# Windowed attention stack on one Trainium2 core: norms of q and k apart, softmax tail moved within VectorE's slot

## The reference

```python
def attn_layer(x, Wqkv, qs, ksc, Wo):              # x is shifted by one token in its upper half of channels
    q, k, v = heads(x @ Wqkv)                      # 16 heads of 64, INNER = 1024
    q = q / max(|q|, 1e-12) * qs                   # |.| over the 64 of a head
    k = k / max(|k|, 1e-12) * ksc
    q = q * cos * scale + rotate_half(q) * sin * scale
    k = k * cos / scale + rotate_half(k) * sin / scale
    out = local_attention(q, k, v)                 # windows of 32 tokens see themselves and the window before
    return out @ Wo
def ffn_layer(x, g, b, W1, b1, W2, b2):            # layer norm, then a gated GELU of 341
    a, gate = split(layernorm(x) * g + b @ W1 + b1)
    return (a * gelu(gate)) @ W2 + b2
for i in range(6):
    x = attn_layer(shift(x), ...) + x
    x = ffn_layer(shift(x), ...) + x
```

## Time and profile before

| | us |
|---|---|
| median of 3 runs | 4362.35 (4358.89 to 4362.66) |
| the profiled execution | 4365.13 |
| its span | 4363.3 |
| PE busy | 3866.2 (89%) |
| DVE busy | 3296.5 (76%) |
| ACT busy | 2534.1 (58%) |
| POOL busy | 2498.8 (57%) |

### The profile page before, as it was taken

The page is one execution under the profiler, slowest core; times in us unless marked ns, Lnnn a source line. Parts: engine busy times, 40 slices in busy tenths (PEclk is TensorE's granted clock), DMA queues, the critical chain, the costliest instruction groups (busy, mean ns, idle before and its releaser), DMA issues. The chain is left out here.

```text
span 4363.3 us, 151598 instructions
## 1 busy us (share of the span) xinstructions
PE 3866.2 (89%) x66488; PEld 2314.4 (53%) x66488; DVE 3296.5 (76%) x4385; ACT 2534.1 (58%) x3236; POOL 2498.8 (57%) x2036
## 2 busy tenths in 40 slices
PE   6887799999999999999778877899999999999997
PEld 3323456665665666665433334566666666666664
DVE  7997777888888787888454436788888878878884
ACT  6885456566665666666324444556566565666654
POOL 0001677777777777777100005786777777777773
PEclk8999999999999999999789998999999999999998
DMA  0001232332323233222000002323323223232221
GB/s 19 1 1 42 72 87 65 85 77 75 83 67 87 73 78 85 62 67 62 17 1 1 1 14 74 92 62 84 81 67 85 73 79 80 73 81 71 66 60 40
DMA packets 165593, 260.83 MB, mean 60 GB/s; under 512 B 58572, under 2 KB 79816, under 8 KB 164936
## 3 DMA queue, kind: packets, MB, share of 16 engines
q1 hardware_dynamic: 164936, 251.13, 22.2%
HBM read 48.61 MB, written 1.05 MB: 11 GB/s over the span
## 5 line engine op out<-in xcount | busy, mean ns | idle before, releaser
L1374 POOL TENSOR_TENSOR f_k_rotated<-f_rope_ak,f_rope_bk 128x1024 f32<-128x1024 f32 x192 | 454.5, 2367 | 288.7 <-DVE f_rope_bk L1429 288.7
L1097 PE MATMUL banks<-f_wqkv,H 128*128 128x512 f32 x1152 | 564.9, 614 | 17.4 <-DVE f_E L1469 9.2
L1097 PE MATMUL banks<-f_wqkv,G 128*128 128x512 f32 x1152 | 551.8, 601 | 0.0
L1426 DVE TENSOR_TENSOR f_rope_aq<-banks,f_rope 128x1024 f32<-128x1024 f32 x192 | 235.1, 1225 | 389.5 <-ACT f_sqq L1284 376.2
L1361 POOL MEMSET f_kT<- 128x256 f32 x2 | 0.6, 311 | 839.9 <-POOLq L514 460.5
L1374 POOL TENSOR_TENSOR f_q_rotated<-f_rope_aq,f_rope_bq 128x1024 f32<-128x1024 f32 x192 | 454.5, 2367 | 29.0 <-DVE f_rope_bq L1429 28.6
L1319 ACT ACTIVATE f_V<-banks 128x1024 f32<-128x1024 f32 x192 | 196.8, 1025 | 418.7 <-PE banks L1097 418.3
L1152 PEld LDWEIGHTS banks<-f_O_T,f_wo 128*128 128x128 f32 x3072 | 372.6, 192 | 98.3 <-issue 94.6
L1152 PE MATMUL banks<-f_O_T,f_wo 128*128 128x128 f32 x3072 | 375.4, 275 | 6.4 <-issue 5.2
L1392 POOL TENSOR_TENSOR f_E<-f_E,f_row_inverse 128x1024 f32<-128x1024 f32 x192 | 368.6, 1920 | 19.8 <-DVE f_row_inverse L1484 19.8
L1386 POOL TENSOR_TENSOR f_q_rotated<-f_q_rotated,f_inverse_norm 128x1024 f32<-128x1024 f32 x192 | 365.2, 1902 | 15.0
(11 more groups left out here) (207 smaller groups left out, 8961.6 us busy)
## 6 DMA issues: line engine op xcount, KB each, us to landing
f_P_T_paired<-f_P_T SPq DMA_DIRECT2D x1536, 64.0 KB
f_V_previous<-f_V SPq DMA_DIRECT2D x192, 384.0 KB, 3.7
f_V_previous<-f_V SPq DMA_DIRECT2D x192, 128.0 KB, 2.4
f_wqkv<-in_L_ffn_Wqkv SPq DMA_DIRECT2D x48, 384.0 KB, 4.1
f_rope<-in_rope SPq DMA_DIRECT2D x24, 512.0 KB, 5.1
f_wo<-in_L_ffn_Wo SPq DMA_DIRECT2D x12, 512.0 KB, 5.4
f_w<-in_L_ffn_W SPq DMA_DIRECT2D x12, 341.0 KB
f_w<-in_L_ffn_W SPq DMA_DIRECT2D x24, 64.0 KB
```

Of the source, the lines that this page charges most:

```text
L1097: mm = nc.tensor.matmul(ps[:, o * BLK:(o + 1) * BLK], xs, w[:, c * INNER + o * BLK:c * INNER + (o + 1) * BLK], start=True, stop=True)
L1374: nc.gpsimd.tensor_tensor(qk[i][:], ra[i][:], rb[i][:], ALU.add).then_inc(radd.sem, 1)
L1426: nc.vector.tensor_tensor(heads_of(ra[i][:]), src, table(2 * i, 0, DH), ALU.mult).then_inc(rot.sem, 1)
```

## The change

Nothing of the arithmetic changes. Four things do:

1. The clamp, the seed, the four refining steps and the use of the norms are made for q and for k apart, on 16 sums each in place of 32. On DVE the sum of q's squares and its clamp stand between the rope of q and the rope of k, those of k after the difference of the scores. On ACT the seed of q stands after the squares of k, ahead of the GELU and of V; the seed of k where the common one was. On POOL the order is add q, refine q, normalise q, add k, refine k, normalise k.
2. The row sum and its inverse leave the end of DVE's slot and stand at the head of the next one, so they serve tile n-2.
3. POOL's multiplication of `E` by the inverse goes with it to the head of POOL's slot, ahead of the add of q.
4. The block transpose of n-2 leaves the place after the rope of q and stands after the clamp of k. On SP the two DMAs of V therefore stand ahead of the eight of the transposed weights.

```diff
-                if live(s - 2):
-                    dve.wait_ge(pn.sem, pn.at(n - 2))
-                    ...
-                    nc.vector.transpose(PT[:].rearrange("p b t -> p (b t)"), E[n % 2][:]).then_inc(ppt.sem, 1)
+                if live(s - 2):
+                    dve.wait_ge(expd.sem, expd.at(n - 2))
+                    nc.vector.tensor_reduce(rs[:], by_side(E[n % 2]).rearrange("p b h w -> p h b w"), AX.XY, ALU.add)\
+                        .then_inc(smd.sem, 1)
...
                 nc.vector.tensor_reduce(ss[n % 2][:, i * HEADS:(i + 1) * HEADS], heads_of(sq[i][:]), AX.X, ALU.add)\
                     .then_inc(red.sem, 1)
+                dve.wait_ge(red.sem, red.at(n, i + 1))
+                h = ss[n % 2][:, i * HEADS:(i + 1) * HEADS]
+                nc.vector.tensor_scalar(h, h, 1e-24, None, ALU.max).then_inc(clamped.sem, 1)
...
+            def seeds(n, i):
+                h = slice(i * HEADS, (i + 1) * HEADS)
+                act.wait_ge(clamped.sem, clamped.at(n, i + 1))
+                act.wait_ge(newton.sem, newton.past(n - 1, 4 * (i + 1)))
+                nc.scalar.activation(lg[:, h], ss[n % 2][:, h], ACT.Ln).then_inc(seeded.sem, 1)
+                act.wait_ge(seeded.sem, seeded.at(n, 2 * i + 1))
+                nc.scalar.activation(y0[:, h], lg[:, h], ACT.Exp, scale=-0.5).then_inc(seeded.sem, 1)
```

More of the change, by code:

```diff
@@ L1380, in _ @@
-                    nc.gpsimd.tensor_scalar(rt[:], rt[:], -0.5, 1.5, ALU.mult, ALU.add).then_inc(newton.sem, 1)
-                    pool.wait_ge(newton.sem, newton.at(n, 3))
-                    nc.gpsimd.tensor_tensor(rn[:], rt[:], y0[:], ALU.mult).then_inc(newton.sem, 1)
-                    pool.wait_ge(newton.sem, newton.at(n))
-                    pool.wait_ge(radd.sem, radd.at(n))
-                    for i in range(2):
-                        nc.gpsimd.tensor_tensor(heads_of(qk[i][:]), heads_of(qk[i][:]),
-                                                over(rn[:, i * HEADS:(i + 1) * HEADS], DH), ALU.mult)\
-                            .then_inc(nrm.sem, 1)
```

66 lines of the change are left out of this document (34 added, 32 removed).

## The result

| | median of all runs, us | lowest to highest | profiled span, us | mean granted clock |
|---|---|---|---|---|
| before | 4362.66 (7 runs) | 4358.89 to 4369.81 | 4363.3 | 0.974 |
| changed | 4335.76 (7 runs) | 4329.61 to 4346.94 | 4333.3 | 0.971 |

The ratio is 0.9939, with a 95% interval of 0.9929 to 0.9949: faster by 27 us where 66 were forecast. The direction was right, the size was not. The kernel before, run beside each group of experiments, had medians from 4360.6 to 4365.1 us, so a difference between the medians of two experiments is good to some 5 us.

What follows compares the result with a forecast made beforehand. The prediction took the path from rope of k through sums, clamp, seed and norms to k's transpose as the bound. 4365.1 - 40 (steady slots) - 26 (fill) = 4299 profiled, so 4296 us median; 8 in 10 within 4185 to 4365.

Steps and rivals of the forecast that it cites:

- What bounds the kernel: Path from rope of k over sums, clamp, seed, refining and norms to k's transpose; at most 1.4 us a slot to gain.
- Head of DVE: Row sum (1.24) and inverse (0.25) at the head of DVE's slot cost nothing; 3.14 us of idleness cover them.
- Queue of q: On DVE the clamp of q waits for POOL's add, ending at 7.9, not 6.8; rope of k starts at 7.87.
- The rival without a meeting: DVE's clamp passes freely beside POOL; mean slot 16.1 us, kernel 4134 us; chance 8%.
- Slot by slot: Steady slots A 16.23, B 16.94, C 18.07, D 16.78: sum 68.02, or 17.0 a slot against 17.23.
- the term 176 x 0.23 = 40: 88 steady slots a call from slot 8 on, two calls, each 0.23 us shorter: 40 us gained.
- DMAs of a moved step: Block transpose 8.6 later moves eight weight issues; the last lands about 23.5, before `values` wants them at 25.3.
- End of a call: The end of a call has no live tile behind it: taken as nothing, bounds 5 us to either side.
- Fill, 2 x 13: First slots of each call, tiles 0 to 7, go from 17.6 to 15.7 us: 13 us a call, 26 in all.
- Slower, DVE loses its turn: In B POOL starts the add of q first, clamp waits 2.3 more: 101 us, 4397; 12% for the slower side.
- Weights late: Paired weights land 2 to 3 us later; decides only if 1.8 more, then one for one; chance 5%.

Runs made afterwards that it cites:

- experiment 8: Changed kernel, clamps kept, with next layer's loads ahead of the paired weights, last row sum a slot earlier, fill pause filled with unread matmuls: 4296.36 us (0.9848).
- Norms apart alone: Kernel before with only sums, clamps, seeds, refining and norms of q and k made apart, nothing moved: 4315.15 us (0.989).

## Why the prediction was partly right

- **What bounds the kernel.** Right. The path over sums, clamp, seed, refining and norms is what the changed kernel shortened: the norm of k ends at 17.69 of the slot instead of 20.2. In the whole run the transposes of k wait 12.6 us for it on PE (121.9 before), and none of that between tile 10 and tile 95.
- **Head of DVE, at no cost.** Right: in A and D the rope of q starts at 3.08 as before, with the inverse of the row sum done by 1.8, and in C it starts at 4.75, where the step said 4.9.
- **Queue of q: the clamp waits for POOL.** Right, in A and D to 0.03 us (in B and C the rope of k starts up to 0.3 earlier than said), and the rule was then shown by changing nothing but the kind of instruction (943, 941 and 170 ns). The rival without a meeting said 4134; taking the meeting away gave 4149 and 4159, and 4129 with the loads ahead as well.
- **Slot by slot, the term 176 x 0.23 = 40.** Right for the clean slots: 67.87 against 68.02. Wrong as a mean: over the whole steady part A took 16.5, B 16.8, C 18.45, D 16.85, together 68.6. By the stretch from tile 10 to 95 the gain was 0.08 a slot where the step said 0.23: 14 us in place of 39. The late loads took 16.5 of the difference (8.1 and 8.4 back with the loads moved). Some 9 us are left, about the grain of the table: the slots behind the rope tables and the two D slots with a lower clock, and A slots that took 16.4 to 16.8 where 16.23 was said.
- **DMAs of a moved step.** This is the step that failed, behind that term. I asked of the later issues only whether the paired weights come in time, and they did. I didn't ask what else stands behind them in SyncE's queue: the next layer's loads moved with them and fell onto `values`, where the stops of PE end with its own instructions and not with data. It cost 16.5 us of the 40.
- **End of a call, nothing, bounds 5.** This term failed as well: 8.5 and 5.7 us were lost, 14 in all, outside its bounds. "No live tile behind it" was true and beside the point: the last tile's own tail had moved behind a slot of feed-forward steps. Made early again, the first call's end is back at 69.8 us (71.7 before); the second, at 74.0, came back only in experiment 8.
- **Fill, 2 x 13.** The sum was right (12.9 and 15.2) by luck. The 17.6 us a slot of the kernel before is a mean over slots that aren't alike: from tile 0 to 4 they took over 18, from tile 4 to 7 they took 17.0. Between tiles 0 and 4 the two calls gained 25 us; between 4 and 7, where the step expected 15.7 a slot, they gained under 1, since five of eight slots took 17.1 with the clock down behind the pause ahead of `out`, which the prediction didn't consider. Slots without a dip took 15.5 to 15.9, as said.
- **Slower, DVE loses its turn.** It happened once. Of the 246 clamps in the trace that take over 0.5 us, 245 overlap one step of POOL and end with it. The other came 0.05 us before POOL's multiplication of `E` ended, waited through the add of q behind it as well, and took 2.40 us (DVE, then POOL):

```profile
2649.06 2.40 DVE L1444 TENSOR_SCALAR f_sum_of_squares<-f_sum_of_squares 128x16 f32<-128x16 f32 x1
...
2649.07 2.36 POOL L1386 TENSOR_TENSOR f_q_rotated<-f_rope_aq,f_rope_bq 128x1024 f32<-128x1024 f32 x1
```

- **Weights late.** Didn't happen; 2.8 us of idle time ahead of `values` name them.
- **The rival that was missing.** That one half might beat the whole. Norms apart alone gives 4315, most likely because a step that looks like a burden, the block transpose between the ropes, keeps the clamp out of POOL's addition.

The changed kernel with the late loads, the last row sum and the pause mended runs at 4296.4 us, 39 us less, so costs of the forecast's size did stand outside the path that I followed. That it hits the forecast of 4296 is luck all the same: its parts are 41, 23 and 1 us where the forecast had 26, 39 and 0, and the matmuls that fill the pause are in no kernel that was forecast.

## What to carry to other kernels

Where two engines share a port, choose the kind of a tiny instruction before its place: in this kernel a clamp of 0.17 us took 1.3 us in A and D ahead of the rope of k as a `tensor_scalar` and 0.17 as a reduce (0.19 as the exact one), which is 176 us of 4336 for the kernel. When a step moves, list everything queued behind it on every queue it uses, follow it through the last iterations of the loop as well as the middle, and check what its removal brings together at the old place.
